# Self attention's scores: three groups over four row tiles and four PSUM banks in place of six blocks over two, with the order of all engines rewritten around them

## What is computed

```python
q = (X @ Wq + bq)   # 64 heads of 16: 4 branches x 16 heads
v = (X @ Wv + bv)
k = tile((X @ Wk + bk), 4 branches)   # 16 heads
q, k = rope(q), rope(k)
scores = einsum('bhtd,bhsd->bhts', q, k) * DH ** -0.5
w = softplus(scores / sqrt(sum(k * k)))
w = where(causal, w, 0)
w = w * sigmoid(SCALE * w)
alpha = 1 / (sum(w) + sinks + 1e-6)
context = einsum('bhts,bhsd->bhtd', w * alpha, v) + sinks * alpha * v_nulls
x = layernorm(x + mean over branches (context @ Wo + bo))
```

## Time and profile before

| | |
|---|---|
| median of 3 runs | 2532.61 us |
| lowest and highest | 2527.84 and 2534.07 us |
| the profiled execution, its own time | 2523.02 us |
| its span, from the first to the last instruction | 2521.4 us |
| mean granted TensorE clock | 0.917 of full speed |
| TensorE busy in the span | 2123.3 us (84%) |
| VectorE, ScalarE, GpSimd busy | 1353.3, 1126.2 and 473.7 us |

### The profile page before, as it was taken

How to read it: one execution, slowest core, us unless ns; L and a number is a source line. 1 busy time by engine, 2 the same in 40 slices (tenths; PEclk the granted TensorE clock), 3 DMA queues, 4 the chain that set the end, 5 groups by cost and what they waited for, 6 DMA issues and landing times. The chain is left out here.

```text
span 2521.4 us, 48525 instructions
## 1 busy us (share of the span) xinstructions
PE 2123.3 (84%) x17362; PEld 1312.1 (52%) x17363; DVE 1353.3 (54%) x3264; ACT 1126.2 (45%) x2404; POOL 473.7 (19%) x533
## 2 busy tenths in 40 slices
PE   1899899865999997867768999999999999864992
PEld 0455555543666664644434555555555555552661
DVE  1677777742555555368873555555555555521223
ACT  0566666632555553235553454444444544420110
POOL 2565555400000001134430000000000000003002
PEclk9799999866999998879989999999999999966996
DMA  5000000024000000000000000000000000035101
GB/s 155 1 2 0 0 0 0 2 60 136 19 18 12 18 12 1 1 1 0 0 6 12 7 7 6 6 12 6 6 6 6 6 7 6 1 106 202 34 29 58
DMA packets 50461, 60.82 MB, mean 24 GB/s; under 512 B 9849, under 2 KB 44974, under 8 KB 49918
## 3 DMA queue, kind: packets, MB, share of 16 engines
q1 hardware_dynamic: 47366, 53.74, 6.9%
q0 software_dynamic: 3008, 5.91, 0.8%
HBM read 51.11 MB, written 8.52 MB: 24 GB/s over the span
## 5 line engine op out<-in xcount | busy, mean ns | idle before, releaser
L2156 DVE CUSTOM_DVE_ANT_0 la_pr<-la_pS,la_mb 100x461 f32<-100x461 f32 x256 | 148.1, 636 | 195.5 <-PE la_pS L2019 195.5
L2001 PE MATMUL la_side<-la_wkv,la_inT 128*128 128x512 f32 (+1 forms) x512 | 242.5, 596 | 0.0
L2257 ACT ACTIVATE la_pr<-la_pr,la_nm 100x461 f32<-100x461 f32 x256 | 171.9, 674 | 134.9 <-DVE la_nm L2156 134.9
L1989 PE MATMUL la_side<-la_inT,la_wkv 128*128 128x461 f32 x512 | 227.3, 566 | 1.3 <-ACT la_inT L2241 0.8
L2265 ACT COPY la_pT<-la_pPT 128x400 f32<-128x400 f32 x256 | 126.1, 493 | 165.4 <-PE la_pPT L2027 164.2
L2027 PEld LDWEIGHTS la_pPT<-io_ident,la_pr 100*128 100x128 f32 x1024 | 110.4, 144 | 148.9 <-issue 105.6
L1029 DVE TENSOR_REDUCE ca_nm<-ca_pS 100x2 f32<-100x722 f32 x128 | 116.1, 907 | 111.7 <-PE ca_pS L916 109.8
L2324 POOL TENSOR_TENSOR la_xb<-io_X,la_bo 100x256 f32<-100x256 f32 x16 | 11.6, 725 | 838.6 <-DVE io_X L2145 838.6
L2027 PE MATMUL la_pPT<-io_ident,la_pr 100*128 100x100 f32 x1024 | 137.6, 258 | 29.7 <-ACT la_pT L2265 18.4
L1101 ACT ACTIVATE ca_pr<-ca_pS,ca_nm 100x361 f32<-100x361 f32 x256 | 129.8, 560 | 64.3 <-DVE ca_nm L1029 62.5
L2118 DVE COPY la_v<-la_side 128x512 f32<-128x512 f32 (+1 forms) x128 | 87.7, 686 | 101.2 <-PE la_side L2001 101.2
(11 more groups left out here) (356 smaller groups left out, 4359.2 us busy)
## 6 DMA issues: line engine op xcount, KB each, us to landing
rf_w<-in_L_ffn_W SPq DMA_DIRECT2D x16, 1024.0 KB, 14.4
ca_cn<-in_ctx SPq DMA_DIRECT2D x16, 256.0 KB, 2.7
la_cn<-in_ctx SPq DMA_DIRECT2D x16, 256.0 KB, 2.8
rows_in<-io_zero SPq DMA_DIRECT2D x20, 128.0 KB, 4.7
rb_xr<-rows_in POOLq DMA_DIRECT2D x20, 128.0 KB, 2.3
rows_out<-rb_yr SPq DMA_DIRECT2D x20, 128.0 KB, 1.7
ea_wcT<-in_t_L_ffn_conv_W SPq DMA_DIRECT2D x1, 2048.0 KB
la_wkv<-in_L_xattn_Wkv SPq DMA_DIRECT2D x1, 2048.0 KB
```

Of the source, the lines that this page charges most:

```text
L1989: last = nc.tensor.matmul(pf[:, 0:SK], wkv[:, k, e * P:(e + 1) * P], inT[:, k, :], start=k == 0, stop=k == KD - 1)
L2001: last = nc.tensor.matmul(pf[0:keys[c], :], inT[:, k, c * P:c * P + keys[c]], wkv[:, k, o:o + 512], start=k == 0, stop=k == KD - 1)
L2156: ins = nc.vector.tensor_tensor_reduce(out=pr[m % 2][:, e, 0:SK], in0=pS[0:T, 2 * (m % 2) + e, 0:SK], in1=mb[b][:, :], scale=-1.0, scalar= ...
L2257: ins = nc.scalar.activation(pr[m % 2][:, e, 0:SK], pr[m % 2][:, e, 0:SK], ACT.Exp, scale=-1.0, bias=nm[m % 2][:, e:e + 1], accum_out=zs[m ...
```

## The change

- `scores` has three groups n = 0, 1, 2. Each uses all four row tiles and all four banks of `pS`. Group 0 holds the late keys of both g (the old blocks 0 and 1), group 1 the early keys of g = 0 (blocks 2 and 3), group 2 those of g = 1 (blocks 4 and 5). Each waits until all blocks of the group before it are masked, and counts s_S once, so three times for a batch. The masks, the sigmoids and the buffers stay in six blocks.
- TensorE: block 1 no longer stands behind `context_summed`, nor block 2 behind the second `q_projected`. Group 1 stands between values 0 and `values_turned` 0, where block 3 was. `v_projected` 1 moves ahead of `values_turned` 1, and group 2 stands behind that, ahead of values 2. `k_turned` moves ahead of `values_turned` 2.
- VectorE: masks 1 ahead of `context_read`; `k_summed` ahead of masks 2; both `v_biased` ahead of `normalised` 1; masks 4 and 5 together behind it; `kT_read` ahead of `normed`; `softplus` 0 from ahead of `normalised` 3 to behind `xT_read`.
- ScalarE: sigmoids 0 and 1 ahead of `values_read` 0, sigmoids 2 and 3 ahead of `values_read` 1, then `values_read` 1 and 2, then sigmoids 4 and 5.

```diff
-                def scores(s, b, c):
-                    if c == 0:
+                def scores(s, b, n):
+                    if n == 0:
                         pe.wait_ge(s_kT, s + 1)
                         pe.wait_ge(s_qT, s + 1)
-                    above(pe, s_sm, s * NCH + (c - 1))
-                    for g in range(KD) if c < 2 else (c // 2 - 1,):
-                        for e in range(2):
-                            j = 2 * (c % 2) + e
+                    above(pe, s_sm, s * NCH + 2 * n)
+                    for g in range(KD) if n == 0 else (n - 1,):
+                        for j in range(NJ):
                             tile = slice(QR * j, QR * (j + 1))
-                            if c < 2:
-                                out, keys, q = pS[:, 2 * (c % 2) + e, g * NBR * TB:(g + 1) * NBR * TB], 1, qT[b][tile, g, :, HK:T]
+                            if n == 0:
+                                out, keys, q = pS[:, j, g * NBR * TB:(g + 1) * NBR * TB], 1, qT[b][tile, g, :, HK:T]
                             else:
-                                out, keys, q = pS[:, 2 * (c % 2) + e, 0:UA], 0, qT[b][tile, g, :, :]
+                                out, keys, q = pS[:, j, 0:UA], 0, qT[b][tile, g, :, :]
...
                 def masked(s, c):
                     if c == 0:
                         above(dv, s_W, s * NPT)
-                    dv.wait_ge(s_S, s * NCH + (c + 1))
+                    dv.wait_ge(s_S, s * NPT + (c // 2 + 1))
...
+                    if F:
+                        kT_read(f, other)
                     if O:
                         normed(o)
-                    if F:
-                        kT_read(f, other)
-                    if S:
-                        softplus(s, par, 0)
                     if V:
                         normalised(v, 3)
                     if N:
                         xT_read(f + 1, par)
                     if S:
+                        softplus(s, par, 0)
                         softplus(s, par, 1)
                         softplus(s, par, 2)
...
                     if V:
                         values_read(v, 1)
-                    if S:
-                        sigmoid(s, par, 3)
-                    if V:
                         values_read(v, 2)
                     if S:
                         sigmoid(s, par, 4)
```

More of the change, by code:

```diff
@@ L403, in body @@
                         context_summed(o)
-                    if S:
-                        scores(s, par, 1)
                     if F:
@@ L411, in body @@
                         q_projected(f, other, 1)
-                    if S:
-                        scores(s, par, 2)
                     if V:
@@ L416, in body @@
                     if S:
-                        scores(s, par, 3)
+                        scores(s, par, 1)
                     if V:
@@ L424, in body @@
                     if S:
-                        scores(s, par, 4)
+                        v_projected(s, par, 1, F)
                     if V:
@@ L428, in body @@
                     if S:
-                        v_projected(s, par, 1, F)
+                        scores(s, par, 2)
                     if V:
                         values(v, other, 2)
-                    if S:
-                        scores(s, par, 5)
-                    if V:
-                        values_turned(v, 2)
                     if F:
@@ L438, in body @@
                     if V:
+                        values_turned(v, 2)
                         values(v, other, 3)
@@ L560, in body @@
                         k_biased(f)
+                    if S:
+                        masked(s, 1)
                     if O:
                         context_read(o)
-                    if S:
-                        masked(s, 1)
                     if F:
@@ L570, in body @@
                         q_biased(f, 1)
+                        k_summed(f)
                     if S:
                         masked(s, 2)
-                    if F:
-                        k_summed(f)
-                    if S:
                         masked(s, 3)
@@ L580, in body @@
                         v_biased(s, par, 0)
-                        masked(s, 4)
+                        v_biased(s, par, 1)
                     if V:
@@ L584, in body @@
                     if S:
-                        v_biased(s, par, 1)
+                        masked(s, 4)
                         masked(s, 5)
@@ L659, in body @@
                         sigmoid(s, par, 0)
+                        sigmoid(s, par, 1)
                     if V:
@@ L662, in body @@
                     if S:
-                        sigmoid(s, par, 1)
                         sigmoid(s, par, 2)
+                        sigmoid(s, par, 3)
                     if V:
                         values_read(v, 1)
-                    if S:
-                        sigmoid(s, par, 3)
-                    if V:
                         values_read(v, 2)
```

7 lines of the change are left out of this document (2 added, 5 removed).

## The result

| | before | after |
|---|---|---|
| median of 4 runs | 2531.63 us | 2497.29 us |
| lowest and highest | 2527.84 and 2534.07 | 2489.95 and 2506.79 |
| the profiled execution, its own time | 2523.02 | 2506.79 |
| mean granted TensorE clock | 0.917 | 0.923 |
| self attention's last instruction ends at | 551.9 | 532.8 |

The direction was right, the size was not.

What follows compares the result with a forecast made beforehand. At full clock, TensorE bounds a batch's head (VectorE close behind) and middle, ScalarE its tail. 8 x 27.1 + 6 x 28.8 = 389.6 against 399.4, some 2 less in the last batches: -12, so 2520 us, range 2503 to 2547.

Steps and rivals of the forecast that it cites:

- The batch at full clock: Self attention batch at 2.4 GHz: 26.9 + 1.49 - 0.58 - 0.71 = 27.1 us, so nothing gained.
- Head: From H to E: VectorE's `cxT` comes later, TensorE waits 2.4 us ahead of `out_projected`; +1.49 us a batch.
- H: Start of scores 0 in a batch, from which the prediction counts times; 315.07 in the earlier trace.
- E: Moment the second Q projection is issued, 324.39 in the earlier trace, H + 9.32.
- The four row tiles: Score groups on TensorE: four tiles side by side keep the next step off for 0.89 us, bounds 0.87 and 1.74.
- Middle: From E to V, TensorE alone: -0.83 for fewer score blocks, a wait of 0.25 ahead of values 1; -0.58 us.
- V: Start of values 2 in a batch, 334.05 in the earlier trace, E + 9.66.
- Tail: From V to the next H, ScalarE: sigmoid 5 right behind sigmoid 4, table load 0.71 us sooner; -0.71 us.
- The number of falls: Batches where TensorE's clock falls to 1.2 GHz: 6 of 14 taken, at 28.8 us each; 5 before, at 31.3.
- Rival 3: No batch has a clock fall: 14 x 27.1 = 379.4 us, kernel at 2511; chance 0.13.
- The last batches: End of self attention, 489 to 552: two score passes are cheaper, some 2 us less.
- The base: Start of the forecast: -12 from the profiled 2523.0 gives 2511; the same difference from the runs' median 2532.6 gives 2520.

Runs made afterwards that it cites:

- the later pair of traces: Unedited second profiles of the changed kernel (median 2498.42 us) and of the kernel before (profiled execution 2525.07 us).
- the last group behind: Changed kernel with the last scores group issued behind values 2 again, not ahead of them; 2519.8 us, ratio 0.9958.
- the first group alone: Kernel before with only score blocks 0 and 1 issued as one group at block 0's place; 2507.85 us, ratio 0.9907.
- the tail kept busy: Kernel before with one unused 512-column matmul more per batch, ahead of the last turn of the values; 2503.04 us, ratio 0.9898.

## Why the prediction was wrong

**The batch at full clock: right.** Forecast 27.1, measured 27.1 to 27.3. By its steps, in the batch from 278.75:
- Head: `out_projected` at H + 8.11 (8.1 forecast), behind a wait of 2.31 (2.4); E at H + 10.87 (10.81). The experiments that undid the two moves measured them: `softplus` 0 costs 1.0 (1.27, less the slack, forecast), masks 1 cost 0.7 (0.66), and with both undone a batch took the 25.5 us that I had named for `cxT` on time (25.6).
- The four row tiles: 0.88 us for a group (0.89). The Trainium skill, "TensorE: Matmul & The Clock Gate", Part 3, has four row tiles gain 3.07 times. The 1.13 that I made of it was an estimate that took the time of a pair for that of one tile alone. The group took 0.88, as long as a pair. No row shows one tile alone, so the 3.07 itself is not tested here.
- Middle: V at E + 8.96 (9.08). The wait of 0.25 ahead of values 1 did not come: they start at E + 4.55.
- Tail: the table load at V + 3.50, not V + 3.27, and the next H at V + 7.43, not 7.14. VectorE's `normalised` (L520) took 0.82 us there in place of 0.42, ahead of masks 4, and the sigmoids end those 0.2 us later. It is the one place where a duration was off. Before, the same operation took 0.79 us one part later (at 310.81); in both kernels a GpSimd operation ran beside it, but others with one beside them took 0.42, and no run tells the cause.
- GpSimd did not bind, as forecast.

**The number of falls: wrong.** This is the step of the sum that failed: "How many batches get one I cannot derive, only bound: 5 of 14 now, and TensorE will idle more ... I take 6." There is one that costs, and two that cost nothing. The one begins behind the new wait, in a batch of 28.6 us, for which I had 28.7. For a fall at the place of before I had 28.9, with a length of 10.2 us taken over from the kernel before; the two of this kind last 3.4 us and their batches take 27.2. So both the number and the price were too high: 380.9 us for fourteen batches in place of 389.6. Rival 3 (no batch falls, 2511) named the case, and I gave it 0.13. Its evidence, four batches of the same work and order with hardly a fall, should have weighed more.

The reason for 6 was the sum of TensorE's idle time over the batch. The runs show that this is the wrong quantity: TensorE idles more in a batch of the changed kernel (5.3 us of 27.2, against 2.9 of 26.8 before) and has no long fall. What the long falls hang on in the loop is the idle tail ahead of scores 0, by the run that only filled its longest spell (long falls gone, over 25 us) and by the run that brought a long spell back (long falls back, 22 us). And that spell I had in hand: it stands in the earlier trace rows, I had named it as what lies ahead of the falls, and my own tail step (sigmoids 0.71 us sooner) shortens the wait, from 1.36 us to 0.71. I costed that step at 0.71 us and did not ask what it does to the spell.

**The last batches: the 2 us did not come.** I had "two score passes are cheaper, some 2 us". In the profiled pair they took 1.0 more, at a mean clock of 0.64 against 0.69; in the later pair of traces they took 59.2 us in both, at 0.71 against 0.74. So the clock took back what less work gave, and one pair does not settle the sign.

**The base: wrong.** "The same difference from 2532.6 gives 2520" carried a sum made for one execution over to the median of others. The sum missed the profiled pair by little, 12 forecast against 16.2 measured: the fourteen batches gave 8.8 more than I had, the first 1.5, while the last batches gave 3.0 less and the stages behind, which no edit touched, took 2.7 more. That the total came so near is in part luck. But I set the profiled execution, which lay below the runs of its kernel, against a median, as if the changed kernel's would lie so too, and its profiled execution lay 9.5 above its median. Of the 22.7 us between my 2520 and 2497.3, some 4 are the sum's, and some 18 are that of the base. So this is the second step that failed, and the larger one: it put the time outside my range. Where those 18 us lie in the executions near the median is not shown, for none of them was profiled. What the traces do show is how far executions differ: the two of before by 7.3 us in self attention (five long falls and seven), the two later ones of before and after stand 33.6 us apart there, and the stages behind it took between 1962.2 and 1973.4 us in the eleven traces.

**What stays open.** Why a fall lasts 10.2 us in one kernel and 3.4 in another. In the kernel with the last group behind, falls at 0.7 to 0.9 us behind scores 0 lasted 10.2 and those at 0.3 and 1.5 lasted 3.4, in batches with the same idle spells as far as the timelines show. With the first group alone they lasted 10.2 at H + 0.5 and 6.8 at H + 1.1 to 1.3. The long falls at the sixteenth scores 0 point the same way: a short spell ahead, little work behind, and 10.2 us or more. So the place at which a fall starts seems to have a part in its length, and what lies behind H too; no run took the two apart. With the tail kept busy the two falls start at H + 1.6 and H + 1.7, not at H + 0.8 or less as in the two traces of before, so that run leaves open whether the tail's idle time sets the length of a fall or only whether one can start right behind scores 0. Nor is it shown why in the kernel before every second batch had one from 225.6 on. The rows give a hint: its falls start at 284.0, 342.1, 400.1 and 458.1, 58.0 us apart, and a batch with a fall and one without take 31.2 + 26.9 = 58.1 together, so each fall meets the batch at nearly the same place as the last one did.

## What to carry to other kernels

Read TensorE's idle spells one by one against the starts of the stretches at half clock, and look at what work stands behind them: the ones that stand ahead of them are what a change should take away, and here even a useless matmul in it paid (over 25 us of 2530). Where executions differ in such stretches, count them in more than one trace before a sum is made on one, and put the distance from trace to median, of both kernels, inside the range. And price each reordering alone: the grouping gave some 50 us with the old orders, while two moves of VectorE's work that came with it cost 23.

## What the runs showed of the hardware that I had not expected

- The clock falls in stretches of 3.4, 6.8, 10.2 us and longer, and a stretch of 3.4 us can be free: at the start of a batch, where TensorE would have waited for VectorE later in any case, the batch took 27.2 us with it and without it.
- Four row tiles with 32 rows each and 400 columns take 0.88 us for eight instructions; two took 0.87 for four.
- More work can be faster: 512 columns more in every batch, in a spell that was idle, took the median from 2531.9 to 2503.0 us.
